# Weighted one-hots of the relational passes on ScalarE instead of VectorE, in a graph network kernel

## Chip, cores and metric

One core of a Trainium2 chip. The time is the device time of one launch in microseconds (us), as the median of three runs.

## What is computed

A graph of N = 3125 nodes with 256 f32 features and 100,000 edges, each with a source, a destination and one of four types. First one graph convolution with a layer norm, then four relational layers, then a last residual with a layer norm:

```python
# first layer
h = x @ W
norm = deg_inv_sqrt[src] * deg_inv_sqrt[dst]
out = segment_sum(h[src] * norm[:, None], dst)
x = layernorm(x + out)
# relational layer, four times, X = x at first
h = einsum('ni,rio->rno', X, W)          # four products per node
msg = h[etype, src] * inv_deg[:, None]   # inv_deg: 1 / edges of this type at dst
agg = segment_sum(msg, dst)
out = agg + X @ root + bias
out = elu(layernorm(out) * gamma + beta)
X = out + X
# at the end
return layernorm(x + X)
```

## The kernel before

**Stages.** The nodes lie in 25 windows of 128. The kernel first sorts the edges by window of the destination, into NT = 806 tiles of 128 slots (0 to about 687 us of the span; nothing in it is changed), and then makes five passes over these tiles: pass q = 0 is the plain layer, q = 1 to 4 are the relational ones. Window j has its last tile at `done_at[j]`, on average every 32.2 tiles.

**A tile.** Tile t of pass q, n = q × 806 + t, goes through four engines:

- POOL gathers 128 feature rows of 1 KB from HBM with one indirect DMA (`gather`, L420) into the ring `msg` of RING = 16 tiles. It waits until the matmul 16 tiles earlier has reported on the semaphore `s_mm`.
- An engine makes the one-hot `emat` (128 slots x 128 nodes of the window; entry = weight of the edge where the destination is that node, else 0) into a ring of BODY = 32 tiles.
- PE multiplies `emat` transposed by `msg` into one of NPS = 4 PSUM banks (`aggregate`, L526). It waits for the one-hot (`s_em`), the gather and for the add four tiles back (`s_acc`).
- VectorE adds the bank to the window's sum in `acc` (`add_tiles`, L963), waiting for this matmul and for its own add before.

**Who makes the one-hots.** In the plain pass (`serve_first`) ScalarE makes them without weight (1 or 0), in two operations: for a batch of HALF = 16 tiles the square of (column number − node) (L667) into `square`, a part of `hout`, then per tile relu(1 − square) (L676), which waits for the matmul 32 tiles back. VectorE makes no one-hots there; it computes each tile's column of `weight` for the later passes (L953). In the relational passes VectorE makes the weighted one-hot in one operation, is_equal then mult (`edge_matrix`, L937), 16 tiles ahead of the add: 16 at the start of the pass, then one in front of each add.

**A window's end.** Once a window is complete, its layer norm, elu, residual and the products for the next pass are done between the tiles of the following windows, as steps of the engines at fixed tile distances from `done_at[j]`. On VectorE: statistics at 0 and 1, reciprocal of the deviation (L1027, waits for ScalarE's root `wsd`) at 4, `centre`, `scale`, `negative` at 5 to 7, `elu` at 10 (waits for the exponential), `residual` at 11. PE: transposes at 15, products (L486) at 18 to 21, which wait for ScalarE's copy `xt` (L619), root product at 22 and 23. ScalarE in a relational pass (`serve_messages`) has nothing but these steps and goes through them in order, each as soon as its semaphore allows: square root (L600), exponential (L611), copies of the new features to `X` (L615) and `xt` (L619), the products out to `hout` and `acc` (L625, L627). Root and exponential each load their function table first. In the plain pass these steps stand between the relus, at their own distances. SP writes each window's features to HBM (`s_hs`), and a pass's first gather waits for all windows of the pass before.

## Time and profile before

| | |
|---|---|
| median of 3 runs | 6666.26 us (6665.17 to 6673.17) |
| profiled execution | 6682.33 us, span 6680.6 us, mean TensorE clock 0.737 of full |
| busy in the span | PE 4180.6 us (63%), PE weight loads 2343.2 (35%), VectorE 3865.1 (58%), ScalarE 1459.7 (22%), POOL 4340.6 (65%) |
| plain pass | 687 to 1882 us |
| relational passes | 1915 to 3077, 3110 to 4271, 4301 to 5462, 5495 to 6650 us |

Busy shares are averages over the span. In the rows below PE is the matmul part of TensorE, PEld its weight loads, DVE is VectorE, ACT ScalarE. "Idle before" is the time an engine stood still in front of the group of instructions, and behind "<-" is what ended most of it: a line of another engine, a DMA, "issue" (nothing that the profile shows) or "remote" (an event whose sender isn't seen). The granted TensorE clock is a share of full speed: 1.00 is 2.4 GHz, 0.50 is 1.2 GHz.

### The profile page before, as it was taken

The page shows a single profiled execution, that of the slowest core. Times are in us where ns is not written, and L with a number is a line of the kernel's source. Part 1 is how long each engine was busy: PE and PEld are TensorE (multiplying, and loading weights), DVE is VectorE, ACT ScalarE, POOL GpSimd, SP SyncE. Part 2 cuts the span into 40 slices and gives each one's busy share as a digit, 9 for nine tenths or more (in the row PEclk, how much of TensorE's full clock was granted, in tenths as well). Part 3 has the DMA queues.
Part 4 walks back from the last instruction along what each step waited for, and adds up shares of the span by engine and source line. Part 5 has one row for each costly group of instructions (what it writes and reads, how often), then busy time and mean ns, then how long its engine had stood idle before and what let it go on. Part 6 is the DMA issues. An engine that isn't in the chain of part 4 may idle for free.

```text
span 6680.6 us, 65433 instructions
## 1 busy us (share of the span) xinstructions
PE 4180.6 (63%) x12629; PEld 2343.2 (35%) x12629; DVE 3865.1 (58%) x10916; ACT 1459.7 (22%) x3865; POOL 4340.6 (65%) x4345
## 2 busy tenths in 40 slices
PE   2888566666656666665666666566665665555554
PEld 2444233333323333333343333333343332333322
DVE  8888677776655455554554554455454444555554
ACT  1666545454401111110111111111111110000000
POOL 1888677776656666665666666566666656666665
PEclk7999677787767777776777777767777766666676
DMA  1000433333343333333333333333333333333333
GB/s 43 1 1 1 149 104 105 102 106 99 97 114 105 100 105 104 100 103 93 101 104 100 104 104 101 99 100 101 104 103 102 103 89 93 92 91 92 91 92 96
DMA packets 280591, 617.13 MB, mean 92 GB/s; under 512 B 77007, under 2 KB 150561, under 8 KB 280152
## 3 DMA queue, kind: packets, MB, share of 16 engines
q0 software_dynamic: 203040, 529.13, 28.6%
q1 hardware_dynamic: 77240, 84.68, 3.9%
q8 instruction: 94, 1.54, 0.1%
q14 instruction: 217, 1.78, 0.1%
HBM read 549.83 MB, written 63.36 MB: 92 GB/s over the span
## 4 chain that ended last, share of the span: by engine, by line
PE 32%; another core or an unknown queue 16%; issue 14%; DVE 9%; DVEq 2%; ACT 1%; DMA 0%; ACTq 0%; SPq 0%
PE bank L526 27%; DVE arena L963 6%; PE bank L486 4%; DVE emat L937 1%; DVEq L963 1%; PE bank L493 1%; PE bank L496 1%; DVEq L947 0%; PE bank L477 0%; DMA msg<-h_table,g_rel 0%; DMA h_table<-hout 0%; DVE found L953 0%; DVE hout L1032 0%; DVE wstats L1018 0%
## 5 line engine op out<-in xcount | busy, mean ns | idle before, releaser
L526 PE MATMUL bank<-msg,emat 128*128 128x256 f32 x8060 | 3168.0, 519 | 2098.7 <-issue 1178.1
L420 POOL DMA_INDIRECT msg<-h_table,g_rel x3224 | 3064.3, 950 | 1703.9 <-issue 740.6
L963 DVE TENSOR_TENSOR arena<-arena,bank 128x256 f32 x4030 | 1686.3, 418 | 2489.6 <-remote 1341.3
L526 PEld LDWEIGHTS bank<-msg,emat 128*128 128x128 f32 x8060 | 1763.3, 248 | 3590.6 <-issue 3085.3
L937 DVE TENSOR_SCALAR emat<-iota,node,weight 128x128 f32<-128x128 f32 x3224 | 1151.4, 359 | 112.3 <-issue 84.9
L420 POOL DMA_INDIRECT msg<-h_table,g_src x806 | 843.5, 1047 | 373.5 <-issue 184.9
L953 DVE SCALAR_TENSOR_TENSOR found<-iota,key,arena 128x512 f16<-128x512 f32 x806 | 600.6, 745 | 63.1 <-issue 49.8
L486 PE MATMUL bank<-w_sb,xt 128*128 128x512 f32 x800 | 498.3, 712 | 146.9 <-ACT xt L619 102.0
L403 POOL DMA_INDIRECT placed_dram<-leaving,idx x300 | 428.2, 1427 | 232.4 <-issue 225.4
L556 PE MATMUL bank<-arena,emat 125*128 125x403 f16 x2000 | 414.7, 338 | 167.8 <-DVE arena L886 167.8
L676 ACT ACTIVATE emat<-hout,ones 128x128 f32<-128x128 f32 x806 | 293.4, 396 | 535.8 <-PE bank L526 349.9
L600 ACT ACTIVATE wsd<-wmv,eps_col 128x1 f32<-128x1 f32 x125 | 36.8, 295 | 1666.3 <-issue 870.1
L625 ACT COPY hout<-bank 128x512 f32<-128x512 f32 x200 | 106.9, 586 | 1036.5 <-remote 527.3
L705 ACT ACTIVATE emat<-emat,arena 125x128 f16<-125x128 f16 x1000 | 303.0, 388 | 10.1 <-DVE emat L865 1.6
L556 PEld LDWEIGHTS bank<-arena,emat 125*128 125x128 f16 x2000 | 160.9, 98 | 324.7 <-DVE arena L886 239.8
L486 PEld LDWEIGHTS bank<-w_sb,xt 128*128 128x128 f32 x800 | 180.4, 232 | 210.3 <-ACT xt L619 122.7
L667 ACT ACTIVATE hout<-iota,neg_node 128x128 f32<-128x128 f32 x806 | 241.5, 387 | 9.7 <-issue 5.5
L611 ACT ACTIVATE hout<-hout 128x256 f32<-128x256 f32 x100 | 41.7, 417 | 746.3 <-DVE hout L1042 442.7
L886 DVE TENSOR_SCALAR arena<-iota,arena 125x806 f16<-125x806 f16 x500 | 195.7, 425 | 0.0
L611 ACT ACT_TABLE_LOAD x100 | 128.3, 1283 | 1.8
L493 PE MATMUL bank<-root_sb,xt 128*128 128x256 f32 x400 | 127.2, 403 | 0.0
L869 DVE TENSOR_TENSOR emat<-iota,arena 125x1024 f16<-125x1024 f16 x101 | 122.8, 1216 | 0.0
(148 smaller groups left out, 1636.8 us busy)
## 6 DMA issues: line engine op xcount, KB each, us to landing
msg<-h_table,g_rel POOLq DMA_INDIRECT x3224
h_table<-hout SPq DMA_DIRECT2D x100, 512.0 KB
msg<-h_table,g_src POOLq DMA_INDIRECT x806
arena<-inv_dram SPq DMA_DIRECT2D x1, 6400.0 KB
placed_dram<-leaving,idx POOLq DMA_INDIRECT x300
w_sb<-in_L_gnn_weights_dram SPq DMA_DIRECT2D x8, 512.0 KB, 5.7
h_table<-hout SPq DMA_DIRECT2D x25, 128.0 KB, 1.7
x_dram<-hout SPq DMA_DIRECT2D x25, 128.0 KB
```

What stands on the lines that cost most here:

```text
L403: pool.indirect_dma_start(out=placed_dram[:, :], out_offset=bass.IndirectOffsetOnAxis(ap=idx[0:EP, n:n + 1], axis=0), in_=leaving[:, n, :] ...
L420: pool.indirect_dma_start(out=msg[:, n % RING, :], out_offset=None, in_=table[:, :], in_offset=bass.IndirectOffsetOnAxis(ap=rows[:, t:t + ...
L486: pe.matmul(win_ps[h][:, :], xt[:, 0, k * P:(k + 1) * P], w_sb[:, k, 2 * h:2 * h + 2, :].rearrange("p r o -> p (r o)"), start=(k == 0), st ...
L526: pe.matmul(agg_ps[n % NPS][:, 0:D], emat[:, n % BODY, :], msg[:, n % RING, :], start=True, stop=True).then_inc(s_mm, 1)
L556: pe.matmul(ps[half][:, 0:HB], slot[:, n, :], tile_hot[:, n, half * HB:(half + 1) * HB], start=False, stop=False)
L667: a = act.activation(square[:, i * P:(i + 1) * P], iota[:, 0:P], ACT.Square, bias=neg_node[:, t:t + 1])
L676: act.activation(emat[:, t % BODY, :], square[:, i * P:(i + 1) * P], ACT.Relu, bias=ones[:, 0:1], scale=-1.0).then_inc(s_em, 1)
L705: a = act.activation(slot[:, n, :], lane_hot[:, b, m, :], ACT.Copy, scale=val[:, bass.ds(i * SU + k, 1)])
L886: dve.tensor_scalar(tile_hot[:, n, :], iota16[0:EP, :], pos_hi[:, bass.ds(t + m, 1)], None, ALU.is_equal).then_inc(s_hot, 1)
L937: dve.tensor_scalar(emat[:, n % BODY, :], iota[:, 0:P], node[:, t:t + 1], weight[:, t:t + 1], ALU.is_equal, ALU.mult).then_inc(s_em, 1)
L953: dve.scalar_tensor_tensor(found[:, t % 2, :, :], key_v, key[:, t:t + 1], inv_v[:, :, bass.ds(w, 1), :].rearrange("p r w d -> p r (w d)"), ...
L963: dve.tensor_tensor(a, a, agg_ps[n % NPS][:, 0:D], ALU.add).then_inc(s_acc, 1)
```

## The change

ScalarE makes the one-hots of all five passes with one function, `edge_matrices(q, work)`, in the manner of the plain pass: 16 squares, then a relu per tile. In a relational pass the relu takes two columns as operands, relu(weight − weight × square), so that it gives the weight where the square is 0 and 0 elsewhere. For this VectorE computes `neg_weight` = −`weight`, one operation on 806 columns at the end of the plain pass, and ScalarE waits for it (`s_nw`) in front of pass 1. VectorE's `edge_matrix` goes, and with it the 16 one-hots at a pass's start. ScalarE's window steps now stand between the relus at fixed indices of `emat`: with at0 = `done_at[j]` + 32, the root at at0 + 3, the exponential at + 9, the last pass's second root at + 15, the copies `X` and `xt` at + 16, the products out at + 25. The ring sizes, the steps of VectorE and PE, the gathers and SP's transfers stay.

```diff
@@ -110,6 +110,7 @@
         wrstd = sb("wrstd", [P, 1])
         wnmr = sb("wnmr", [P, 1])
         neg_node = sb("neg_node", [P, NT])
+        neg_weight = sb("neg_weight", [P, NT])
         square = hout[:, 1:3, :].rearrange("p a b -> p (a b)")
         assert HALF * P == 2 * R * D
 
@@ -259,6 +261,7 @@
         SORT0 = SU
         ONE0 = 1
         NFIRST, NSTEP, NFIN = 3, 5, 5
+        HALVES = -(-NT // HALF)
 
         block = ctx.enter_context(nc.Block())
 
@@ -631,18 +634,53 @@
                 act.activation(wsd[:, :], wmv[:, 1:2], ACT.Sqrt, bias=eps_col[:, :]
                                ).then_inc(s_fsd, 1)
 
+            def edge_matrices(q, work):
+
+
+                for t0 in range(0, NT, HALF):
+                    tiles = range(t0, min(NT, t0 + HALF))
+                    made = q * NT + t0
+                    if made:
+                        act.wait_ge(s_em, made)
+                    for i, t in enumerate(tiles):
+                        a = act.activation(square[:, i * P:(i + 1) * P], iota[:, 0:P],
+                                           ACT.Square, bias=neg_node[:, t:t + 1])
+                    a.then_inc(s_sq, 1)
+                    act.wait_ge(s_sq, q * HALVES + t0 // HALF + 1)
+                    for i, t in enumerate(tiles):
+                        n = q * NT + t
+                        if t in work:
+                            work[t]()
+                        if n >= BODY:
+                            act.wait_ge(s_mm, MM0 + n + 1 - BODY)
+                        bias, scale = ((weight[:, t:t + 1], neg_weight[:, t:t + 1]) if q else
+                                       (ones[:, 0:1], -1.0))
+                        act.activation(emat[:, n % BODY, :], square[:, i * P:(i + 1) * P],
+                                       ACT.Relu, bias=bias, scale=scale).then_inc(s_em, 1)
+                for at in sorted(work):
+                    if at >= NT:
+                        work[at]()
+
             def serve_messages(q, last=False):
+                number, work = {}, {}
+
+                def features(j):
+                    number[j] = window_at(mybir.EngineType.Activation, j)
+                    window_features(q * NW + j, number[j])
+                    window_transposed(q * NW + j)
+
                 for j in range(NW):
-                    n = q * NW + j
-                    v = window_at(mybir.EngineType.Activation, j)
-                    window_sd(n)
-                    window_exp(n - NW)
+                    n, at0 = q * NW + j, done_at[j] + BODY
+                    work[at0 + 3] = lambda n=n: window_sd(n)
+                    work[at0 + 9] = lambda n=n: window_exp(n - NW)
                     if last:
-                        final_sd(j)
+                        work[at0 + 15] = lambda j=j: final_sd(j)
                     else:
-                        window_features(n, v)
-                        window_transposed(n)
-                        window_products_out(n, v)
+                        work[at0 + 16] = lambda j=j: features(j)
+                        work[at0 + 25] = lambda n=n, j=j: window_products_out(n, number[j])
+                if q == 1:
+                    act.wait_ge(s_nw, 1)
+                edge_matrices(q, work)
 
             def serve_first():
                 number = {}
@@ -659,26 +697,7 @@
                     work[at0 + 8] = lambda j=j: normalised(j)
                     work[at0 + 12] = lambda j=j: window_transposed(j)
                     work[at0 + 24] = lambda j=j: window_products_out(j, number[j])
-                for t0 in range(0, NT, HALF):
-                    tiles = range(t0, min(NT, t0 + HALF))
-                    if t0:
-                        act.wait_ge(s_em, t0)
-                    for i, t in enumerate(tiles):
-                        a = act.activation(square[:, i * P:(i + 1) * P], iota[:, 0:P],
-                                           ACT.Square, bias=neg_node[:, t:t + 1])
-                    a.then_inc(s_sq, 1)
-                    act.wait_ge(s_sq, t0 // HALF + 1)
-                    for i, t in enumerate(tiles):
-                        if t in work:
-                            work[t]()
-                        if t >= BODY:
-                            act.wait_ge(s_mm, MM0 + t + 1 - BODY)
-                        act.activation(emat[:, t % BODY, :], square[:, i * P:(i + 1) * P],
-                                       ACT.Relu, bias=ones[:, 0:1], scale=-1.0).then_inc(s_em, 1)
-                for at in sorted(work):
-                    if at >= NT:
-                        work[at]()
-
+                edge_matrices(0, work)
 
             copy_transpose(0, 0)
             with act.Fori(0, NC - 1) as c:
@@ -931,12 +950,6 @@
             dve.wait_ge(s_h0, NW)
             dve.memset(acc, 0.0).then_inc(s_acc, ACC0)
 
-            def edge_matrix(q, t):
-
-                n = q * NT + t
-                dve.tensor_scalar(emat[:, n % BODY, :], iota[:, 0:P], node[:, t:t + 1],
-                                  weight[:, t:t + 1], ALU.is_equal, ALU.mult).then_inc(s_em, 1)
-
             inv_v = inv_b.rearrange("p (r w d) -> p r w d", r=R, w=NW)
             key_v = iota[:, :].rearrange("p (r d) -> p r d", r=R)
 
@@ -954,8 +967,6 @@
                             found[:, t % 2, :, :], key_v, key[:, t:t + 1],
                             inv_v[:, :, bass.ds(w, 1), :].rearrange("p r w d -> p r (w d)"),
                             ALU.is_equal, ALU.mult, accum_out=weight[:, t:t + 1])
-                    elif t + HALF < NT:
-                        edge_matrix(q, t + HALF)
                     dve.wait_ge(s_mm, MM0 + n + 1)
 
                     dve.wait_ge(s_acc, ACC0 + n)
@@ -963,6 +974,9 @@
                     dve.tensor_tensor(a, a, agg_ps[n % NPS][:, 0:D], ALU.add).then_inc(s_acc, 1)
                     if t + 1 in work:
                         work[t + 1]()
+                if q == 0:
+                    dve.tensor_scalar(neg_weight[:, :], weight[:, :], -1.0, None, ALU.mult
+                                      ).then_inc(s_nw, 1)
                 for at in sorted(work):
                     if at > NT:
                         work[at]()
@@ -1113,8 +1127,6 @@
                 if q == 0:
                     dve.wait_ge(s_inv_b, 16)
                 else:
-                    for t in range(HALF):
-                        edge_matrix(q, t)
                     dve.wait_ge(s_ev, q * NW + ONE0)
                 add_tiles(q, window_steps(q))
```

(The declaration of the semaphore `s_nw` is left out.)

ScalarE in a relational pass, before: one window, from its first step to its last copy, and the next one's number. Names are output<-input; the shape is the output's.

```order
L600 ACT_TABLE_LOAD
L600 ACTIVATE wsd<-wmv,eps_col 128x1 [waits s_var]
L611 ACT_TABLE_LOAD
L611 ACTIVATE hout<-hout 128x256 [waits s_min]
L615 ISA [waits s_xn]
L615 COPY X<-hout 128x256
L619 COPY xt<-bank 128x256 [waits s_tw]
L625 COPY hout<-bank 128x512 [waits s_hs,s_hm]
L625 COPY hout<-bank 128x512
L627 ISA
L627 COPY arena<-bank 128x256
L270 TENSOR_LOAD order_i
```

And now, from before a square root to after the next batch of squares (L603 is the root, L614 the exponential, L646 the square, L658 the relu):

```order
L646 ACTIVATE hout<-iota,neg_node 128x128 [waits s_em]
L646 ACTIVATE hout<-iota,neg_node 128x128 x15
L658 ACTIVATE emat<-hout,weight,neg_weight 128x128 [waits s_mm,s_sq]
L658 ACTIVATE emat<-hout,weight,neg_weight 128x128 [waits s_mm] x5
L603 ACT_TABLE_LOAD
L603 ACTIVATE wsd<-wmv,eps_col 128x1 [waits s_var]
L658 ACTIVATE emat<-hout,weight,neg_weight 128x128 [waits s_mm] x6
L614 ACT_TABLE_LOAD
L614 ACTIVATE hout<-hout 128x256 [waits s_min]
L658 ACTIVATE emat<-hout,weight,neg_weight 128x128 [waits s_mm] x4
L646 ACTIVATE hout<-iota,neg_node 128x128 [waits s_em]
L646 ACTIVATE hout<-iota,neg_node 128x128 x15
```

The root and its table load, which followed the preceding window's copies at once, stand behind a batch of 16 squares and six relus here, and the exponential six relus later. How many relus lie between the squares and the root differs from window to window, from 0 to 15.

VectorE in a relational pass, before: from the end of a window, where its number is read (L270) and its statistics begin (L1018), two adds on.

```order
L270 TENSOR_LOAD order_i
L1018 ISA [waits s_acc]
L1018 BN_STATS wstats<-arena 128x6
L947 TENSOR_LOAD win_i
L937 TENSOR_SCALAR emat<-iota,node,weight 128x128
L963 ISA [waits s_acc,s_mm]
L963 TENSOR_TENSOR arena<-arena,bank 128x256
L1023 BN_AGGR wmv<-wstats 128x2 [waits s_step]
L937 TENSOR_SCALAR emat<-iota,node,weight 128x128
L963 ISA [waits s_acc,s_mm]
L963 TENSOR_TENSOR arena<-arena,bank 128x256
```

And the same place now, with L1032 the statistics, L1037 their aggregate and L974 the add:

```order
L273 TENSOR_LOAD order_i
L1032 ISA [waits s_acc]
L1032 BN_STATS wstats<-arena 128x6
L974 ISA [waits s_acc,s_mm]
L974 TENSOR_TENSOR arena<-arena,bank 128x256
L1037 BN_AGGR wmv<-wstats 128x2 [waits s_step]
L974 ISA [waits s_acc,s_mm]
L974 TENSOR_TENSOR arena<-arena,bank 128x256
```

The one-hot in front of every add is gone; the window's steps stand at the same adds as before.

## Rows read from the trace of the kernel before

**Rows 1.** Windows view, plain and relational pass: us, then each engine's busy us (instructions).
```profile
687.00:1882.00 1195.00, 772.37 (x1970) 396.28 (x1970) 856.41 (x2491) 593.67 (x1777) 842.68 (x806) 0.75 0.37 107
3110.00:4271.00 1161.00, 748.75 (x1970) 435.69 (x1971) 577.36 (x1773) 127.11 (x212) 766.06 (x806) 0.72 0.36 103
```

**Rows 2.** Groups by line, POOL, plain pass, then relational: busy, mean ns | idle, releasers.
```profile
L420 POOL DMA_INDIRECT msg<-h_table,g_src x806 | 843.5, 1047 | 373.5 <-issue 184.9 <-PE bank L526 121.0 <-remote 46.1
...
L420 POOL DMA_INDIRECT msg<-h_table,g_rel x806 | 766.5, 951 | 426.9 <-issue 187.0 <-remote 113.2 <-PE bank L526 94.7
```

**Rows 3.** Windows view of L963's adds, slices of 4 us: DVE busy (count), TensorE clock, DMA.
```profile
5828.00:5832.00 4.00, 2.53 (x7) 0.54 0.33 98
5832.00:5836.00 4.00, 2.08 (x5) 1.00 0.35 100
...
5840.00:5844.00 4.00, 0.42 (x1) 0.50 0.40 114
...
5848.00:5852.00 4.00, 1.26 (x3) 0.50 0.19 49
```

**Rows 4.** Timeline, slow part of rows 3: start, us, engine, operation [idle before].
```profile
5842.79 1.19 PE L526 MATMUL bank<-msg,emat 128*128 128x256 f32 x2 [3.05 <-issue]
...
5850.11 0.94 POOL L420 DMA_INDIRECT msg<-h_table,g_rel  x1 [2.60 <-remote]
```

**Rows 5.** Timeline of VectorE, fast adds with one window step between.
```profile
3020.82 0.41 DVE L963 TENSOR_TENSOR arena<-arena,bank 128x256 f32 x1
3021.15 0.42 DVE L1053 SCALAR_TENSOR_TENSOR hout<-hout,X 128x256 f32<-128x256 f32 x1
3021.48 0.34 DVE L937 TENSOR_SCALAR emat<-iota,node,weight 128x128 f32<-128x128 f32 x1
3021.74 0.41 DVE L963 TENSOR_TENSOR arena<-arena,bank 128x256 f32 x1
...
3022.37 0.42 DVE L963 TENSOR_TENSOR arena<-arena,bank 128x256 f32 x1
```

**Rows 6.** Timeline of VectorE, end of a pass, no one-hots left.
```profile
4276.13 0.42 DVE L963 TENSOR_TENSOR arena<-arena,bank 128x256 f32 x1 [0.22 <-PE bank L526]
4276.77 0.42 DVE L963 TENSOR_TENSOR arena<-arena,bank 128x256 f32 x1 [0.22 <-PE bank L526]
```

**Rows 7.** Groups by line, whole kernel: count, busy, mean ns | idle before.
```profile
L937 DVE TENSOR_SCALAR emat<-iota,node,weight 128x128 f32<-128x128 f32 x3224 | 1151.4, 359 | 112.3 <-issue 84.9 <-ACT arena L627 25.7
...
L676 ACT ACTIVATE emat<-hout,ones 128x128 f32<-128x128 f32 x806 | 293.4, 396 | 535.8 <-PE bank L526 349.9 <-remote 113.1 <-issue 68.2
...
L611 ACT ACT_TABLE_LOAD x100 | 128.3, 1283 | 1.8
...
L611 ACT ACTIVATE hout<-hout 128x256 f32<-128x256 f32 x100 | 41.7, 417 | 746.3 <-DVE hout L1042 442.7 <-issue 303.6
...
L600 ACT ACTIVATE wsd<-wmv,eps_col 128x1 f32<-128x1 f32 x125 | 36.8, 295 | 1666.3 <-issue 870.1 <-DVE wmv L1023 759.5 <-DVE wmv L989 36.7
...
L606 ACT ACTIVATE hout<-hout,wnmr,wrstd 128x256 f32<-128x256 f32 x25 | 15.0, 598 | 13.8 <-DVE wnmr L996 7.0 <-issue 6.8
```

**Rows 8.** Timeline of ScalarE, plain pass: a batch of squares, relus behind it.
```profile
748.71 4.78 ACT L667 ACTIVATE hout<-iota,neg_node 128x128 f32<-128x128 f32 x16
753.52 0.99 ACT L676 ACTIVATE emat<-hout,ones 128x128 f32<-128x128 f32 x3
```

**Rows 9.** Timeline at a pass boundary: ScalarE's last copy, POOL's first gather.
```profile
3105.85 0.39 ACT L627 COPY arena<-bank 128x256 f32 x1
3106.26 1.28 ACT L600 ACT_TABLE_LOAD   x1
...
3110.00 0.94 POOL L420 DMA_INDIRECT msg<-h_table,g_rel  x1 [31.96 <-DMA h_table<-hout]
```

**Rows 10.** Groups by line, PE at the products, plain pass, then relational.
```profile
L486 PE MATMUL bank<-w_sb,xt 128*128 128x512 f32 x200 | 132.6, 754 | 46.8 <-ACT xt L619 43.3 <-DVE arena L963 3.4
...
L486 PE MATMUL bank<-w_sb,xt 128*128 128x512 f32 x200 | 120.2, 690 | 29.8 <-ACT xt L619 19.2 <-issue 10.6
```

More of the change, by code:

```diff
@@ L217, in build_program @@
         s_em = sem("s_em")
+        s_nw = sem("s_nw")
         s_mm = sem("s_mm")
```

## The prediction

> **What bounds the kernel now.** I read the stretches of the passes first, then what POOL does in one pass, then a few microseconds of each kind inside a pass. The plain pass takes 1195 us and a relational one 1161, and in neither is any engine busy throughout: in the relational pass VectorE works 577 us, PE 749, POOL 766, ScalarE only 127 [rows 1]. POOL, the longest, issues 806 gathers of 0.95 us each and is idle 427 us, of which 187 are "issue" [rows 2]. Its gathers follow each other at best every 0.95 + 0.30 = 1.25 us, that is 806 × 1.25 = 1007 us; the other 154 us of the pass are waits for a free row of the `msg` ring of 16. The pace is 1161/806 = 1.44 us a tile. To save time, the change must shorten those 154 us; VectorE's busy time as such bounds nothing.
>
> When does the ring fill up? Counting VectorE's adds in slices of 4 us shows two regimes [rows 3]: seven, five, then one add in each of three slices (one of them is shown), then three. In the fast regime the adds work off what has piled up; in the slow one a matmul's report reaches its waiters late: PE stands idle 3.05 us although its tiles have landed, and VectorE waits with it, until POOL has stood still for 2.60 us at the full ring [rows 4]. The pattern repeats through every pass; these 24 us hold one of it, at 24/18 = 1.33 us a tile near the mean of 1.44. So 15 of the 18 adds in it fall into the fast regime, 3 into the slow, which lasts more than half of the time. No VectorE work lies in the way of the slow regime.
>
> **The fast regime.** An add follows an add after 0.64 us with the one-hot between them (3021.74 to 3022.37) [rows 5], and also after 0.64 at the end of a pass where no one-hots are left to make [rows 6]. The add waits for the one before it anyway, and the one-hot of 0.36 us [rows 7] lies in that wait. Taking away the 3224 one-hots, 1151 us of work by their row, is thus worth nothing beside a plain add. Only where a window step also stands between two adds does the interval grow, to 0.92 [rows 5]; with the step alone I put it at 0.67, since the step of 0.42 takes about the one-hot's place.
>
> **The change, part by part.**
> 1. VectorE without one-hots: 0.92 − 0.67 = 0.25 us at each of 8 steps, in each of 100 windows of the relational passes, for the fast share 15/18 ≈ 0.8: **−160 us**. Bounds: 0 if what is gained is only waited again at the full ring, −200 if all steps gain.
> 2. ScalarE's own load. A batch of 16 squares takes 4.78 us, 0.30 each; relus follow each other at 0.33 [rows 8]. The new relu has two pointer operands. None of the trace has just these, but two pointers on 256 columns take 598 ns where none takes 417 [rows 7], so 0.09 each: the relu goes from 396 to about 490 ns, its cadence from 0.33 to 0.42. With the window's copies and tables (127/806 = 0.16 us a tile [rows 1]) that is 0.88 us a tile against 1.44. ScalarE doesn't become the bound: cover of 0.56 us a tile. In the fast regime, though, tiles go at 0.64, and there it falls behind; the emat ring of 32 covers that for the one-hots, which are made a ring ahead.
> 3. ScalarE's other steps aren't made ahead. The window's square root now stands at the one-hot that waits for the third matmul behind the window, possibly just behind a batch of 16 squares that can't be interrupted. With k relus between, ScalarE is through after 4.78 + 0.42 k + 1.28 + 0.29 (table load and root, [rows 7]), or 6.4 + 0.42 k. The load counts in full: before, it ran in idle time straight after the preceding window's copies [rows 9]. VectorE comes to the reciprocal that wants the root after (k + 5) × 0.64 + 2 × 0.28 for two steps = 3.8 + 0.64 k (PE being three banks ahead, my assumption). So it stalls 2.6 us at k = 0, 0.22 less with every k, nothing from 12 on: 1.0 us on average over 16 positions. The exponential, six tiles later, has the same distance to its user and can meet the next batch: together 1.0 to 2.1 a window. I take 1.5, as a root's stall covers some of the exponential's: 1.5 × 100 × 0.8 = **+120 us**. Bounds 0 (the stalls fall into slow stretches, or the time is POOL's anyway) and +170.
> 4. The copies of `xt`, on which the window's products wait. PE lost 46.8 us at its products in the plain pass, where ScalarE already makes one-hots, and 29.8 in a relational one [rows 10]: 17 us a pass, and I count 0.4 of it, since more than half of the time is the slow regime's, where PE idles anyway [rows 3]: 4 × 17 × 0.4 = **+30 us**, bounds 0 and +68.
> 5. `neg_weight`: one operation on 806 columns, once. The one-hot's 128 columns take 0.36 us [rows 7], so it is between 0.36 and 806/128 × 0.36 = 2.3 us: **+1**. The wait on it in front of pass 1 is hidden by the write of the last features.
> 6. The pass boundaries: after the last copy at 3106.2 POOL's first gather starts at 3110.0 [rows 9], and the first matmul wants it landed. ScalarE's 16 squares and first relu, 4.78 + 0.5 us, end at 3111.5, before that. VectorE's 16 one-hots there were hidden too. **0**; were they not hidden, 4 × 5 = 20 us.
>
> SP's queue and POOL's see no instruction more or less, and none is moved past a DMA.
>
> **Sum.** −160 + 120 + 30 + 1 = −9 us on a profiled execution of 6682.33, which lies 16 us (0.24%) over the median of 6666.26. On the median: 6666 − 10 = **6656**. By its bounds alone (−200 to 0; 0 to +170; 0 to +68; 0 to +21) the forecast's own range is 6600 to 6720.
>
> A rule for exactly this choice: the Trainium skill ("ScalarE: Activation LUTs", Rules for kernel authors) says to use VectorE, not ScalarE, for relu and multiplications. Here the trace has 0.36 us on VectorE against 0.30 + 0.42 on ScalarE, so it agrees on the price, but what counts is where the price lies; by the rule alone the change would lose.
>
> **Rivals.**
> - **A, faster: the slow regime gets rarer.** In the plain pass, with one-hots on ScalarE, POOL's gathers take 1047 ns [rows 2], so 806 × 1.35 = 1086 of 1195 us, and only 109 us are ring waits against 154 elsewhere. If that is because VectorE doesn't make the one-hots, the relational passes lose 45 us each: 6666 − 180 = **6486**. For it: these 109. Against: in the plain pass VectorE is busy with another product per tile, and slower gathers alone fill the ring more rarely. Far beyond lies the bound at which all ring waits go, 6666 − 4 × 154 = 6050. A neighbouring mechanism would be that VectorE's one-hots hold POOL up: the mean gather with them is 951 ns, lower than the 1047 without, so no sign of it in their length. The Trainium skill ("SBUF — State Buffer", Who interferes with whom) says that VectorE's 2-port modes, which `tensor_scalar` can enter, block GpSimd for the whole instruction; by that rule the gathers should now become shorter.
> - **B, slower: ScalarE's lateness isn't absorbed.** VectorE then stands at the reciprocal, waiting for the root, POOL at the full ring behind it. The place is the square root behind a batch of squares and its table load; it decides once the mean lateness is above the saving of item 1, 0.25 × 8 = 2 us a window less the xt copies, so from some 1.5 us a window. The passes then take what the plain one takes: 4 × (1195 − 1161) = +136, **6802**. For it: ScalarE gets 0.8 us a tile in a stretch where tiles go at 0.64. Against: POOL's 1.25 a tile leave slack.
> - **C, nothing shows.** What VectorE gains in the fast regime it waits again for the next gathers, and the same hides ScalarE's lateness: **6666**, between 6655 and 6680.
>
> **Chances.** Forecast with its own range 0.45 (in it as much below as above no change, since its two large terms nearly cancel), A 0.25, B 0.20, C 0.10. A measurement of this kernel can tell about 0.2%, 13 us. Faster by more: A, and 0.17 of the forecast, 0.42. Within: C and 0.12, 0.22. Slower: B and 0.16, 0.36. The range from A's 6486, rounded, to B's 6802 leaves out the 50 to 100 us beyond either of them: 6480 to 6810.
>
> **What would show it.** Right: adds at 0.64 us plain, as before, and 0.67 with a step; relus of about 490 ns; 1 to 2 us of VectorE's idle time a window put down to `wsd` or the exponential's tile; POOL's gathers still 950 ns and slow stretches with the same 3 us; PE's idle time before the products at 47 us a pass. Wrong: ring waits on POOL nearer 109 us a pass than 154 (A), VectorE stalls above 2 us a window with passes near 1195 us (B), relus of over 0.6 us, matmuls that wait for `emat` from ScalarE in the middle of a pass, or gathers of another length.

## The result and the profile after

The change makes the kernel slower: 6774.98 us (6769.6 to 6780.93, 4 runs) against 6668.17 (6665.17 to 6673.17, 4 runs), ratio 1.0155, interval 1.0143 to 1.0168. I had forecast 6656 with a range up to 6810 and 0.36 for slower. The time fell into the range, by rival B and not by the forecast. The profiled spans are 6680.6 and 6770.8, so 90 of these 107 us are to be found between the two traces (the profiled execution before lies 16 us over its median, the one after 2 us under). The ratios here and below are estimated over each series and can differ by up to 0.0009 from the quotient of its two medians.

They lie in the first three relational passes. First the waits of POOL and PE there: PE at the products (L489, before L486), POOL at its gathers (L423), pass 2. Columns: count | busy us, mean ns | idle before, what ended it.

```profile
L423 POOL DMA_INDIRECT msg<-h_table,g_rel x806 | 766.9, 952 | 454.0 <-issue 171.9 <-PE bank L529 148.9 <-remote 101.5
...
L489 PE MATMUL bank<-w_sb,xt 128*128 128x512 f32 x192 | 139.6, 819 | 174.1 <-ACT xt L622 127.9 <-remote 25.4 <-DVE arena L974 10.9
...
L1041 DVE RECIPROCAL wrstd<-wsd 128x1 f32<-128x1 f32 x24 | 3.9, 163 | 42.1 <-ACT wsd L603 23.8 <-issue 18.2
```

Against [rows 10] PE stands 174 us in front of the products instead of 29.8 (24 windows here, 25 there), that is 7 us a window instead of 1.2. POOL's idle time went from 427 us [rows 2] to 454, with gathers as long as before (952 ns). VectorE waits 42 us for the root, 1.75 a window. From first gather to first gather a pass takes 1221.7 us, the last one of these two lines less the first; before, 4300.36 − 3110.00 = 1190.4:

```profile
3140.01 0.95 POOL L423 DMA_INDIRECT msg<-h_table,g_rel  x1 [31.72 <-DMA h_table<-hout]
...
4328.31 0.94 POOL L423 DMA_INDIRECT msg<-h_table,g_rel  x1 [0.30 <-issue]
4361.73 0.95 POOL L423 DMA_INDIRECT msg<-h_table,g_rel  x1 [32.47 <-DMA h_table<-hout]
```

The passes' gathers extend over 1200, 1188 and 1187 us instead of 1162, 1161, 1162; the last pass, without products, over 1159 instead of 1155, the plain one over 1183 instead of 1195 (its program is the same; why it is shorter stays open), and the four stretches between passes are 7 us longer in all: 90 + 4 − 12 + 7 = 89 us, of 90. The whole kernel's groups:

```profile
L423 POOL DMA_INDIRECT msg<-h_table,g_rel x3224 | 3065.2, 951 | 1804.4 <-issue 717.8
...
L974 DVE TENSOR_TENSOR arena<-arena,bank 128x256 f32 x4030 | 1690.3, 419 | 3317.1 <-remote 1270.4
...
L658 ACT ACTIVATE emat<-hout,weight,neg_weight 128x128 f32<-128x128 f32 x3224 | 1421.9, 486 | 1771.0 <-remote 766.0
L646 ACT ACTIVATE hout<-iota,neg_node 128x128 f32<-128x128 f32 x4030 | 1206.6, 387 | 56.2 <-remote 37.6
...
L489 PE MATMUL bank<-w_sb,xt 128*128 128x512 f32 x800 | 569.4, 805 | 595.4 <-ACT xt L622 426.3
```

ScalarE is busy 56% instead of 22%. Its one-hots don't hold PE up: in the first tiles of a relational pass they stand 4 tiles or more ahead of PE, and from the 29th tile to the 32nd from the end 19 or more. The profile puts 77 us of PE's idle time before the matmuls of pass 2 down to the relus, but for 65 of them PE starts within 0.5 us of the end of the add four tiles before, which the matmul waits for as well, and the one-hot lay ready.

The last pass already says that neither ScalarE's load nor the late root makes most of the loss. There ScalarE is busy 675 of 1160 us and VectorE waits 56 us for roots, but there are no copies of `xt` and no products, and the pass is 3.5 us longer than before.

The loss is at `xt`. One window in order of time, all engines but PE's weight loads (columns: start, us, engine, line, [idle before <- what ended it]):

```profile
3319.88 0.38 PE L480 MATMUL bank<-ident,hout 128*128 128x128 f32 x2
...
3320.10 1.46 PE L529 MATMUL bank<-msg,emat 128*128 128x256 f32 x6
...
3324.07 0.49 ACT L658 ACTIVATE emat<-hout,weight,neg_weight 128x128 f32<-128x128 f32 x1 [3.79 <-remote]
3324.19 0.42 DVE L974 TENSOR_TENSOR arena<-arena,bank 128x256 f32 x1 [3.61 <-remote]
...
3329.70 0.49 ACT L658 ACTIVATE emat<-hout,weight,neg_weight 128x128 f32<-128x128 f32 x1 [5.13 <-remote]
...
3329.93 0.95 POOL L423 DMA_INDIRECT msg<-h_table,g_rel  x1 [3.07 <-remote]
3330.22 4.78 ACT L646 ACTIVATE hout<-iota,neg_node 128x128 f32<-128x128 f32 x16
...
3335.44 0.41 ACT L618 COPY X<-hout 128x256 f32 x1 [0.44 <-ACT hout L646]
3335.75 0.36 ACT L622 COPY xt<-bank 128x256 f32<-128x256 f32 x1
...
3336.17 1.22 PE L489 MATMUL bank<-w_sb,xt 128*128 128x512 f32 x1 [14.60 <-ACT xt L622]
```

PE transposes the window at 3319.88 and does the three matmuls behind it by 3321.6. Then it needs `xt`. ScalarE could copy at once, but its copies come at at0 + 16, behind relus that wait for the report of just these matmuls. The slow regime holds the reports back: the relus start at 3324.07 (3.79 us of waiting) and 3329.70 (5.13 us), the second once POOL had stood still for 3.07 us. Then comes a batch of 16 squares, 4.78 us, and only then the two copies. PE has been idle for 14.60 us.

This is a window of the dearest kind. Windows end every 806/25 = 32.24 tiles and a batch comes every 16, so the windows' steps meet the batches at nearly the same place every time: in the trace 0 relus lie between the batch and the `xt` copy in the first four windows of a pass, 1, 2, 3 and 4 in the next sixteen by fours, 5 in three, and the last two windows are copied after the last relu. Over the three passes PE's idle time before a window's first product is 12.9 us on average with 0 relus between, 8.9 with 1, 6.7 to 6.0 with 2 to 5, and 1.0 in the last two windows. The square root has 3 to 8 relus between the batch and itself, and not 0 to 15 as said ahead of the prediction.

### The profile page after: what moved, and what is told of

It reads as the page before. It is cut to its first block, busy times and chain, and to the rows that moved or that the text cites. A ratio compares the mean times of both kernels' runs of the same rounds, so it can differ in the third digit from the quotient of the medians.

```text
span 6770.8 us, 68851 instructions
## 1 busy us (share of the span) xinstructions
PE 4100.4 (61%) x12629; PEld 2306.8 (34%) x12629; DVE 3075.8 (45%) x7693; ACT 3792.9 (56%) x10313; POOL 4342.8 (64%) x4345
## 4 chain that ended last, share of the span: by engine, by line
PE 33%; ACT 20%; another core or an unknown queue 14%; issue 13%; DVE 6%; DVEq 2%; ACTq 0%
PE bank L529 23%; ACT hout L646 9%; PE bank L489 7%; ACT emat L658 7%; DVE arena L974 5%; PE bank L496 1%; DVE found L966 1%; PE bank L499 1%; DVEq L974 1%; ACT L603 1%; ACT L614 1%; DVEq L960 1%; ACT hout L628 0%; ACT xt L622 0%
## 5 line engine op out<-in xcount | busy, mean ns | idle before, releaser
L423 POOL DMA_INDIRECT msg<-h_table,g_rel x3224 | 3065.2, 951 | 1804.4 <-issue 717.8
L529 PE MATMUL bank<-msg,emat 128*128 128x256 f32 x8060 | 3042.4, 503 | 1819.7 <-issue 926.1
L974 DVE TENSOR_TENSOR arena<-arena,bank 128x256 f32 x4030 | 1690.3, 419 | 3317.1 <-remote 1270.4
L529 PEld LDWEIGHTS bank<-msg,emat 128*128 128x128 f32 x8060 | 1718.5, 241 | 3251.8 <-issue 2196.2
L658 ACT ACTIVATE emat<-hout,weight,neg_weight 128x128 f32<-128x128 f32 x3224 | 1421.9, 486 | 1771.0 <-remote 766.0
L646 ACT ACTIVATE hout<-iota,neg_node 128x128 f32<-128x128 f32 x4030 | 1206.6, 387 | 56.2 <-remote 37.6
L423 POOL DMA_INDIRECT msg<-h_table,g_src x806 | 844.9, 1048 | 360.3 <-issue 190.6
L489 PE MATMUL bank<-w_sb,xt 128*128 128x512 f32 x800 | 569.4, 805 | 595.4 <-ACT xt L622 426.3
L658 ACT ACTIVATE emat<-hout,ones 128x128 f32<-128x128 f32 x806 | 294.4, 397 | 523.0 <-PE bank L529 325.2
L489 PEld LDWEIGHTS bank<-w_sb,xt 128*128 128x128 f32 x800 | 198.7, 262 | 683.1 <-ACT xt L622 510.4
L713 ACT COPY idx<-arena 125x3 int32 (+1 forms) x100 | 19.3, 193 | 246.8 <-DMA placed_dram<-leaving,idx 170.5
L562 PE MATMUL bank<-arena,emat 125*128 125x100 f16 x800 | 117.1, 207 | 0.0
```

The source lines that it names most:

```text
L423: pool.indirect_dma_start(out=msg[:, n % RING, :], out_offset=None, in_=table[:, :], in_offset=bass.IndirectOffsetOnAxis(ap=rows[:, t:t + ...
L489: pe.matmul(win_ps[h][:, :], xt[:, 0, k * P:(k + 1) * P], w_sb[:, k, 2 * h:2 * h + 2, :].rearrange("p r o -> p (r o)"), start=(k == 0), st ...
L529: pe.matmul(agg_ps[n % NPS][:, 0:D], emat[:, n % BODY, :], msg[:, n % RING, :], start=True, stop=True).then_inc(s_mm, 1)
L646: a = act.activation(square[:, i * P:(i + 1) * P], iota[:, 0:P], ACT.Square, bias=neg_node[:, t:t + 1])
L658: act.activation(emat[:, n % BODY, :], square[:, i * P:(i + 1) * P], ACT.Relu, bias=bias, scale=scale).then_inc(s_em, 1)
L974: dve.tensor_tensor(a, a, agg_ps[n % NPS][:, 0:D], ALU.add).then_inc(s_acc, 1)
```

## The experiments

The kernels ran in several series, each time beside the kernel before. That took 6668 to 6678 us in the series called S below (the late reports of [rows 4] are seen there), 6617 in one, and 5947 to 5948 in the two called F. The series were on chips of different numbers, but the number 8 stands both at a series S and at a series F, so it isn't shown that the chip makes the difference: "chip S" and "chip F" name what the kernel before took. Ratios are compared within S or within F only, across two or three series of kind S.

How often reports are late tells S from F. I counted the adds in front of which VectorE stood still for over 0.5 us and which start over 2 us after the profile's end of their matmul: 808 of the 3224 relational adds before and 732 with the change on S, 4 with the change on F. TensorE's clock doesn't explain them: its mean over the 808 stretches is 0.77 of full, and over the relational passes with products 0.72.

### Where ScalarE's steps stand (chip S)

```diff
-                        work[at0 + 16] = lambda j=j: features(j)
+                        work[at0 + 10] = lambda j=j: features(j)
```

> The changed kernel with one edit: ScalarE's copies X and xt stand at at0 + 10 instead of at0 + 16, so the relu in front of them waits for the matmul 9 tiles behind the window and not 15; PE's products stay at 18. Theory 'late copies' (the loss is PE standing at its products for xt, because the copy is queued behind a relu that waits for a matmul only two or three tiles before those products, and behind a batch of squares): PE's idle time before the products falls from 174 us a pass to 30 to 60, and the time by 70 to 110 us, to 6665 to 6705. Theory 'load' (ScalarE has too much work in the fast regime, wherever the copies stand): unchanged, 6760 to 6790. Theory 'late root' (VectorE's reciprocal waits for the root): unchanged too.

Ratio 1.0028 (1.0016 to 1.0039), 6699.87 us. Then all ScalarE steps 8 indices earlier:

```diff
-                    n, at0 = q * NW + j, done_at[j] + BODY
+                    n, at0 = q * NW + j, done_at[j] + BODY - 8
```

> The changed kernel with all of ScalarE's relational window steps 8 indices earlier (root at at0 - 5, exponential at at0 + 1, copies at at0 + 8, products out at at0 + 17). 'Late copies' and 'late root' together: PE's wait for xt and VectorE's wait for the root (42 us a pass before the reciprocal) both go, 6600 to 6680, and at least 10 us below the run with the copies alone. 'Load': 6760 to 6790. If only the copies matter: the same as the run with the copies alone, within 10 us.

Ratio 1.0033 (1.0022 to 1.0045), 6703.52 us. Pass 2 of the copies alone, then of all early, PE at the products and VectorE at the reciprocal:

```profile
L489 PE MATMUL bank<-w_sb,xt 128*128 128x512 f32 x200 | 125.5, 717 | 65.2 <-issue 32.9 <-ACT xt L622 30.9 <-DVE arena L974 1.4
...
L1041 DVE RECIPROCAL wrstd<-wsd 128x1 f32<-128x1 f32 x25 | 4.1, 163 | 60.1 <-ACT wsd L603 48.3 <-issue 11.8
```

```profile
L423 POOL DMA_INDIRECT msg<-h_table,g_rel x806 | 766.6, 951 | 433.0 <-issue 189.6 <-remote 122.7 <-PE bank L529 87.7
...
L489 PE MATMUL bank<-w_sb,xt 128*128 128x512 f32 x200 | 122.1, 699 | 50.7 <-ACT xt L622 38.3 <-issue 11.7 <-DVE arena L974 0.8
...
L1041 DVE RECIPROCAL wrstd<-wsd 128x1 f32<-128x1 f32 x25 | 3.9, 156 | 0.4 <-ACT wsd L603 0.4
```

The copies alone take PE's wait from 174 to 65 us in pass 2 and four fifths of the loss away: "late copies" holds, and "load" falls as the cause of the loss. ScalarE has the same instructions in all three kernels and is busy 703, 696 and 680 us in pass 2. The root, late by 60 us in the first, isn't late in the second (0.4 us), and the time doesn't move: VectorE's wait for the root costs nothing. Both edits do two things at once: the copies wait for a report 6 or 8 tiles earlier, and 8 to 15 relus now lie between the batch and the copy instead of 0 to 5 (again without the last two windows). No run separates the two in a relational pass; the plain pass does, as shown under item 4 below.

What is left is 0.3%, and it is clear of zero. Each relational pass is still 4 to 7 us longer than before. Which part of the change costs them wasn't tested on S, so some 20 us of the price of ScalarE's one-hots are unexplained.

### What makes the copy late (chip S)

The kernel before, with only a gate in front of ScalarE's copies, and then with a batch of squares behind the gate:

```diff
+                        act.wait_ge(s_mm, MM0 + q * NT + min(NT, done_at[j] + 16))
+                        for i in range(HALF):
+                            act.activation(square[:, i * P:(i + 1) * P], iota[:, 0:P],
+                                           ACT.Square, bias=neg_node[:, i:i + 1])
                         window_features(n, v)
```

> The kernel before (one-hots on VectorE, no relus on ScalarE in relational passes), with one wait more: in front of the copies X and xt of the first three relational passes ScalarE waits for the report of the matmul 16 tiles behind the window. 'Late copies' with the report as its cause: PE's idle time before the products rises from 30 to 80 or more us a pass and the time by 20 to 80 us, 6690 to 6750. If instead the squares and relus queued in front of the copy make the loss, and not the report waited for: 6660 to 6680.

The gate alone: ratio 1.0017 (1.0006 to 1.0029), PE waiting 63 us in pass 2. Both rises are smaller than forecast: 12 us in time where 20 to 80 were expected, and a wait below the 80 us.

> The kernel before with the gate and 16 idle squares in front of the copies. On a chip with the slow regime: if report and batch together make the loss 1.010 to 1.018 and 7 to 8 us of PE waiting a window; if the relus are needed under 1.006. Without it: 1.0016 to 1.002, as measured.

Gate and squares: ratio 1.0273 (1.0247 to 1.0299), with VectorE's one-hots and no relus at all; more than the 1.018 expected, with 8.2 us of waiting a window in pass 2. Here the batch stands between report and copy in every window, in the changed kernel in the first four of a pass. Pass 2 of it:

```profile
L420 POOL DMA_INDIRECT msg<-h_table,g_rel x806 | 769.4, 955 | 491.4 <-PE bank L526 187.4 <-issue 173.2 <-remote 90.5
...
L486 PE MATMUL bank<-w_sb,xt 128*128 128x512 f32 x200 | 147.1, 830 | 205.3 <-ACT xt L619 152.6 <-remote 34.5 <-issue 18.2
```

And the changed kernel with squares in batches of 8 (three places of `HALF` in `edge_matrices` and `HALVES` become 8):

> The changed kernel with squares in batches of 8. On a chip with the slow regime: if the batch of squares makes the loss 1.007 to 1.012; if the report in front of the copies does, 1.014 to 1.016. Without it: 0.999, as measured.

Ratio 1.0075 (1.0053 to 1.0098):

```profile
L489 PE MATMUL bank<-w_sb,xt 128*128 128x512 f32 x200 | 134.5, 764 | 90.7 <-ACT xt L622 65.0 <-issue 14.2 <-DVE arena L974 11.6
```

PE's wait in pass 2 and the extent of its gathers rise together, but not in proportion, over the kernels on S: 30 us and 1161 (before), 51 and 1166 (all early), 63 and 1164 (gate), 65 and 1164 (copies early), 91 and 1178 (batches of 8), 174 and 1188 (the change), 205 and 1220 (gate and squares). The change with spare one-hots on VectorE, below, lies off this row with 142 us and 1205: what a wait costs also depends on how fast the engines catch up after it, and gate and squares has VectorE's one-hots too. Halving the batch takes half of the loss. So the report alone is cheap, and report and batch together are dear. A batch without the gate wasn't tried, so what it would cost alone on S stays open.

### What VectorE's one-hots cost (chip S)

A weighted one-hot in front of each relational add, as before, into a part of `xt` that nobody reads, once in the changed kernel and once in the one with all steps early:

```diff
+                    elif t + HALF < NT:
+                        dve.tensor_scalar(spare[:, t % 4 * P:(t % 4 + 1) * P], iota[:, 0:P],
+                                          node[:, t:t + 1], weight[:, t:t + 1],
+                                          ALU.is_equal, ALU.mult)
```

> The changed kernel, with VectorE still making a weighted one-hot in front of each relational add, into a buffer that nobody reads. If VectorE's one-hots cost something beside its steps (my term of -160 us): 6850 to 6950. If they lay wholly in waits, as one rival has it: 6765 to 6790.

Ratio 1.0201 (1.0176 to 1.0225), 0.0046 over the change: 31 us, across two series whose intervals don't meet. Neither theory: not 160, and not nothing.

> All ScalarE steps early, with the spare one-hots on VectorE. On a chip with the slow regime (kernel before at some 6670): 'absorbed' ratio 1.003 to 1.006, the same as without spare one-hots (1.0033); 'credit' 1.02 to 1.03. On a chip without it: 1.000, as measured.

Ratio 1.0048 (1.0035 to 1.0061), against 1.0033 without: 0.0015, 10 us, and the intervals overlap. POOL in pass 2, to be compared with 433.0 us of idle time above:

```profile
L424 POOL DMA_INDIRECT msg<-h_table,g_rel x806 | 765.1, 949 | 435.7 <-issue 195.9 <-remote 110.5 <-PE bank L530 97.0
```

The spare one-hots do to VectorE what the prediction said. With one of them and a window step between, an add follows an add after 0.93 us in this kernel, as in [rows 5]:

```profile
3185.49 0.42 DVE L978 TENSOR_TENSOR arena<-arena,bank 128x256 f32 x1
3185.83 0.42 DVE L1064 SCALAR_TENSOR_TENSOR hout<-hout 128x256 f32<-128x256 f32 x1
3186.16 0.34 DVE L972 TENSOR_SCALAR xt<-iota,node,weight 128x128 f32<-128x128 f32 x1
3186.42 0.41 DVE L978 TENSOR_TENSOR arena<-arena,bank 128x256 f32 x1
```

Over pass 2 the median of such intervals is 0.98 us with spare one-hots and 0.73 without. So the whole 0.25 us a step is given back, and the time moves by some 10 us, by the intervals at most some 20, and not by 160. Behind a PE that has stood still the one-hots are worth 31; that a faster VectorE helps to catch up there is my reading, and no run separates it.

### The chip without late reports (chip F)

Three of these kernels ran on F first, as did the one with 12 outstanding gathers below.

> The kernel with all ScalarE steps early (6703.5 us; before in those rounds 6678.1, ratio 1.0033), and a spare one-hot by VectorE in front of each relational add into a buffer that nobody reads. This is the price of VectorE's one-hots with the late copies out of the way. Theory 'credit' (0.25 us at 8 steps of 100 windows, 160 us): ratio to before 1.02 to 1.03. Theory 'absorbed' (what VectorE gains is waited again at the full ring): ratio 1.003 to 1.006. The late copies left in, it cost 43 us.

Ratio 1.0002 (0.9992 to 1.0011).

> The changed kernel with squares in batches of 8 instead of 16, copies left at at0 + 16. Half as long a batch can stand in front of the copies: if the batch of squares makes the loss, PE's idle time before the products falls by 1 to 2.4 us a window and the time by 20 to 60 us (ratio 1.007 to 1.012). If the report of the matmul in front makes it, it stays at 1.014 to 1.016.

Ratio 0.9991 (0.9982 to 1.0001).

> The kernel before with the same gate as in the earlier run (a wait for the report of the matmul 16 tiles behind the window in front of the copies, ratio 1.0017) and behind it 16 squares of 4.78 us whose results nobody reads. If report and batch together make the changed kernel's loss, PE waits 7 to 8 us a window at its products and the time rises to a ratio of 1.010 to 1.018. If the relus behind which the copies queue are needed for it: under 1.006.

Ratio 1.0020 (1.0010 to 1.0030). In a second series on F, beside the changed kernel, the three gave 1.0002, 0.9987 and 1.0016. So only gate and squares costs something here, some 10 us. From the last gather of a relational pass to the first of the next it takes 31.5 to 32.1 us, and 28.2 to 29.5 in the changed kernel on F; its relational passes are 1 to 2.5 us longer. The changed kernel itself:

> The changed kernel itself, unedited. The last call's chip ran the kernel before in 5948 us, 720 us less than the first chip: its relational passes show 1 to 3 us of ring waits each instead of about 155, and no slow regime. Where the kernel before takes 5948: theory 'the loss needs the slow regime' (late matmul reports in front of the copies) expects a ratio of 0.998 to 1.003; theory 'the loss is ScalarE's backlog' 1.01 or more. Where it takes some 6670: 1.014 to 1.017 as measured.

5943.99 us, ratio 0.9992 (0.9983 to 1.0002). Pass 2 of the changed kernel there, by engines (PE, PEld, DVE, ACT, POOL, clock, DMA share, GB/s), and two of its groups:

```profile
2829.00:3838.00 1009.00, 774.17 (x1988) 407.25 (x1988) 391.55 (x993) 711.52 (x1813) 761.72 (x805) 0.77 0.41 118
```

```profile
L423 POOL DMA_INDIRECT msg<-h_table,g_rel x805 | 761.7, 946 | 245.2 <-issue 148.0 <-PE bank L529 97.2
...
L489 PE MATMUL bank<-w_sb,xt 128*128 128x512 f32 x200 | 130.4, 743 | 42.9 <-ACT xt L622 42.7 <-DMA msg<-h_table,g_rel 0.2
...
L1041 DVE RECIPROCAL wrstd<-wsd 128x1 f32<-128x1 f32 x25 | 4.1, 163 | 33.8 <-ACT wsd L603 33.8
```

The window begins just after the pass's first gather and ends after its last; the gathers take 1008 us, and 806 × 1.25 = 1007 is what POOL needs. ScalarE's steps are late here too, PE waits 43 us and VectorE 34, and neither reaches the time: POOL's idle time is all 0.30 us between gathers, so the ring's slack absorbs them. So the loss needs what S has and F hasn't, of which the traces show the late reports; "backlog" by itself costs nothing.

### How deep a ring is needed

All steps early, and POOL stopping at 12 outstanding gathers instead of 16:

```diff
-                    pool.wait_ge(s_mm, MM0 + n + 1 - RING)
+                    pool.wait_ge(s_mm, MM0 + n + 1 - 12)
```

> All ScalarE steps early and POOL stopping at 12 outstanding gathers. On a chip with the slow regime: if a slow stretch ends once POOL has stood still, ring waits a pass stay near 157 us or fall, ratio 0.99 to 1.006; if the ring's depth covers the slow stretches, 1.02 or more. Without it: 0.999, as measured.

Ratio 0.9998 (0.9988 to 1.0008) on S, 0.0035 below the same with 16 (of another series); on F 0.9991 (0.9981 to 1.0001). Its passes are as long as with 16 (1167 us against 1166 in pass 2), but between them fewer tiles are left over; the last gather of pass 2 and the first of pass 3, with 12, then with 16:

```profile
4262.73 0.95 POOL L423 DMA_INDIRECT msg<-h_table,g_rel  x1 [0.50 <-remote]
4290.66 0.95 POOL L423 DMA_INDIRECT msg<-h_table,g_rel  x1 [26.99 <-DMA h_table<-hout]
```

```profile
4269.13 0.95 POOL L423 DMA_INDIRECT msg<-h_table,g_rel  x1 [0.30 <-issue]
4299.21 0.95 POOL L423 DMA_INDIRECT msg<-h_table,g_rel  x1 [29.14 <-DMA h_table<-hout]
```

27.9 us against 30.1 here, and 109 against 130 over the four boundaries. The kernel before wasn't run with 12, so a tie with it at 16 doesn't show that the one-hots are free here. With 8 outstanding the boundaries should shorten further, and both kernels below should beat the kernel before where reports are late:

> The kernel before with one edit: POOL stops at 8 outstanding gathers instead of 16. With 12 (all steps early) a pass kept its 157 us of ring waits, but the stretch from a pass's last gather to the next pass's first fell from 33 to 27 us, since fewer tiles are left to work off. Theory 'depth doesn't matter' on a chip with the slow regime: passes of 1160 to 1170 us, stretches between them at 20 to 24 us instead of 32, ratio 0.993 to 0.997. If 8 tiles (10 us of gathers) are too few to cover the root and the copies: ring waits rise, 1.005 or more. Without the slow regime: 0.998 to 1.002.

> One-hots on ScalarE with all its steps early, squares in batches of 8, POOL stopping at 8 outstanding. On a chip with the slow regime: 'absorbed' (where the one-hots are made is worth nothing either way once the copies are early) expects the same as the kernel before with 8, within 0.3%: 0.993 to 0.999. If ScalarE's chain still costs: 1.002 or more. Without the slow regime: 0.997 to 1.000.

These two ran in the series between, with the kernel before at 6617.43 us: 0.9997 (0.9987 to 1.0006) and 0.9996 (0.9987 to 1.0006). Reports are late there too: 148 to 150 us of pass 2 are ring waits. The two tie with each other, as "absorbed" has it, but also with the kernel before, which neither forecast for late reports had; its trace in that series wasn't taken, so where the shorter boundaries (26 us in the first) went stays open. No version here beats the kernel before by more than its interval on S or in this series; on F batches of 8 did so once, at 0.9987 (0.9977 to 0.9997).

## Why the prediction was wrong

Two terms of the sum failed. Item 1, −160 us, was a saving that isn't on the path, and item 4, +30 us, was about a third of the loss that the copies of `xt` really make. Item 3, +120 us, wasn't on the path either, and it was luck that items 1 and 3 nearly cancelled: with item 3 alone at 0 the same sum gives 6537 us, with item 1 alone at 0 it gives 6817.

- **What bounds the kernel: held.** Ring waits of POOL set the time; where they are missing (chip F) the pass is 806 × 1.25 us.
- **Item 1, VectorE without one-hots, −160 us: failed.** The interval was right to the hundredth, plain adds stay at 0.64 (0.63 in the last two lines) and one with a step between takes 0.67:

```profile
2037.01 0.42 DVE L974 TENSOR_TENSOR arena<-arena,bank 128x256 f32 x1 [0.22 <-PE bank L529]
2037.35 0.42 DVE L1060 SCALAR_TENSOR_TENSOR hout<-hout 128x256 f32<-128x256 f32 x1
2037.68 0.41 DVE L974 TENSOR_TENSOR arena<-arena,bank 128x256 f32 x1
2038.01 0.42 DVE L1067 SCALAR_TENSOR_TENSOR hout<-hout,X 128x256 f32<-128x256 f32 x1
2038.35 0.41 DVE L974 TENSOR_TENSOR arena<-arena,bank 128x256 f32 x1
2038.98 0.42 DVE L974 TENSOR_TENSOR arena<-arena,bank 128x256 f32 x1 [0.22 <-issue]
```

  But it doesn't lie on the path. Spare one-hots bring the long intervals back and cost 10 us with the copies early, not 160. I multiplied the saving by the share of adds in the fast regime, as if the fast regime's length were the time's; its adds only catch up with a PE that will be stopped by the next late report. The value lies near the lower bound I gave, 0.
- **Item 2, ScalarE's load: held.** The new relu takes 486 ns (490 forecast), ScalarE is busy 703 of 1188 us in a pass, and the move of the copies took four fifths of the loss at the same load. The 0.3% left on S may be the load's.
- **Item 3, the late root, +120 us: the wait was right, its price not.** 42.1 us in 24 windows are 1.75 a window for the root alone, and 0.2 more for the exponential, against 1.5 for both. The mean over 16 positions of the batch was wrong, as the root always stands 3 to 8 relus behind it: by the item's own formula, 2.6 − 0.22 k, that is 0.8 to 1.9 us. And two steps at 0.28 us each don't fit item 1, whose 0.67 leaves 0.03 for a step without a one-hot. Taking the waits away changed nothing (1.0028 with them, 1.0033 without).
- **Item 4, the `xt` copies, +30 us with 68 as the bound: failed, and this is the loss.** I took PE's wait from the plain pass, 1.9 us a window, as the nearest row, and that row is a mean over two kinds of windows. In the plain pass as in the others the products come two tiles behind the report that the copy's relu waits for, but there the `xt` copy stands at at0 + 12. So in the first 16 windows 12 to 15 relus lie between the batch and the copy, and PE waits 0.7 us on average; in the next seven only 0 or 1 do, and it waits 5.0. One product of each kind, with the batch and the copy of the second, in the plain pass of the kernel before:

```profile
769.51 2.07 PE L486 MATMUL bank<-w_sb,xt 128*128 128x512 f32 x2 [0.83 <-ACT xt L619]
...
1527.83 4.78 ACT L667 ACTIVATE hout<-iota,neg_node 128x128 f32<-128x128 f32 x16
1532.64 0.37 ACT L619 COPY xt<-bank 128x256 f32<-128x256 f32 x1
1533.06 2.08 PE L486 MATMUL bank<-w_sb,xt 128*128 128x512 f32 x2 [6.77 <-ACT xt L619]
```

  At at0 + 16 the relational passes have 0 to 5 relus between in 23 of 25 windows: 7.3 us a window in pass 2. The passes' gathers took 28 us more there, and 91 in three passes. Why 0 relus between cost 12.9 us a window in the relational passes and 6.0 in the plain one before wasn't tested; in the plain pass VectorE alone needs 856/806 = 1.06 us a tile [rows 1], so ScalarE falls less far behind than where tiles go at 0.64. The item also counts four passes, but only three of the changed passes make products, so 3 × 17 = 51 us would have been its bound.
- **Items 5 and 6: held.** `neg_weight` takes 0.57 us. From the last gather of a pass to the first of the next it takes 36.7, 32.7, 33.4 and 32.8 us, against 32.8, 32.9, 29.9 and 32.6 before.
- **The range.** The forecast's own range of 6600 to 6720 doesn't follow from the bounds named beside it: added up, they give 6466 to 6925.
- **The rivals.** A fell: ring waits rose and didn't fall; gathers stayed at 951 ns without VectorE's one-hots, so nothing in their length had been blocked; before, the 2338 that overlap a VectorE one-hot and the 886 that don't both have a median of 946 ns. The Trainium skill ("SBUF — State Buffer", Who interferes with whom) expects a lock between VectorE's 2-port modes and GpSimd; no run here shows one in these gathers. B had the sign, the size (136 forecast, 107 measured) and one of its two places: the root stood in it as the place, and `xt` only in the sum. Its condition, a mean lateness above 1.5 us a window, was met and decided nothing. As to the Trainium skill's rule to use VectorE for relu ("ScalarE: Activation LUTs", Rules for kernel authors): the price it warns of was there (0.30 + 0.42 us for 0.36) and cost nothing on F (0.9992) and at most the 0.3% left on S; what cost was the queue behind it.

## What to carry to other kernels

Work moved to an idle in-order engine delays whatever that engine serves, and the delay is not the moved work's own length: ask for each step on it what the instruction in front of it waits for, and how far ahead of its user it stands. Put steps that somebody waits for ahead of the batches of prefetched work, and see where they fall in the batches' rhythm: here 32.24 tiles against 16 put nearly every copy right behind a batch. Time saved on an engine that only catches up after stalls was worth little here: 10 to 31 us, where 160 were forecast.

## What the runs showed of the hardware

The same program took 5947, 6617 and 6668 to 6678 us in different series. Gathers (946 to 955 ns on average) and the fast adds (0.63 to 0.64 us) are the same in all; what differs is the ring waits, 150 to 157 us a relational pass before on S and 1 to 5 in the kernels traced on F, with the late matmul reports. Ring waits are about the same at 12 and at 16 outstanding gathers on S (161 and 160 us in pass 2), so a ring of 12 neither cures nor worsens them. What causes the late reports wasn't found.
